# A fused attention and mixture-of-experts kernel: VectorE makes the last block's digits and squares, its rows are loaded in quarters, and the last transposes stand ahead of two down projections

## The reference

```python
y = _moe_mlp(hidden_states, sg_w, su_w, sd_w)
for i in range(E):                                    # E = 16, K = D // 2 = 96
    gate_feature = hidden_states * pe[i] @ gate_w + gate_b
    gate_weight, gate_idx = jax.lax.top_k(gate_feature, K)
    gate_weight = jax.nn.softmax(gate_weight, axis=-1)
    gathered = jnp.take_along_axis(hidden_states, gate_idx, axis=-1)
    y = y + _moe_mlp(gathered * gate_weight, eg_w[i], eu_w[i], ed_w[i])
yn = layernorm(y) * ln_g + ln_b
return jax.nn.silu(yn @ m1_w + m1_b) @ m2_w + m2_b    # added to the residual outside
```

## Time and profile before

| | us |
|---|---|
| median of 3 runs | 2607.87 |
| lowest and highest of them | 2597.53, 2609.46 |
| the profiled execution, its time | 2605.05 |
| the profiled execution, its span | 2603.2 |

### The profile page before, as it was taken

The page is one execution under the profiler, slowest core; times in us unless marked ns, Lnnn a source line. Parts: engine busy times, 40 slices in busy tenths (PEclk is TensorE's granted clock), DMA queues, the critical chain, the costliest instruction groups (busy, mean ns, idle before and its releaser), DMA issues.

```text
span 2603.2 us, 48218 instructions
## 1 busy us (share of the span) xinstructions
PE 2285.7 (88%) x11466; PEld 1244.9 (48%) x11466; DVE 2494.4 (96%) x13314; ACT 1701.2 (65%) x4090; POOL 1791.9 (69%) x2165
## 2 busy tenths in 40 slices
PE   6788989999988889889998889899889988887888
PEld 4555545454444454445544445445445454443445
DVE  5897999999999999999999999999999999999983
ACT  3354676776776667676667767667676666666563
POOL 1245777777786677777767777767768777676683
PEclk8688999988999799999899999998998988989798
DMA  3021222222221222221222122222221222121211
GB/s 107 18 56 27 53 52 61 46 50 55 53 62 44 47 58 46 57 56 44 53 52 61 45 53 50 57 50 56 51 53 49 46 50 61 43 57 46 50 50 26
DMA packets 124767, 133.58 MB, mean 51 GB/s; under 512 B 39923, under 2 KB 112638, under 8 KB 124486
## 3 DMA queue, kind: packets, MB, share of 16 engines
q1 hardware_dynamic: 123174, 128.02, 21.1%
q0 software_dynamic: 880, 1.62, 0.2%
q10 hardware_dynamic: 432, 0.86, 0.1%
HBM read 102.58 MB, written 27.87 MB: 50 GB/s over the span
## 4 chain that ended last, share of the span: by engine, by line
DVE 74%; PE 12%; DMA 4%; POOL 4%; ACT 3%; issue 3%; SPq 0%; DVEq 0%; ACTq 0%; POOLq 0%
DVE idx L647 26%; DVE keys L649 25%; DVE vals L643 22%; PE ps L1281 3%; DMA rows<-digit_d 2%; PE ps L1338 1%; PE ps L1362 1%; DMA digit_d<-dcode 1%; PE ps L1294 1%; PE ps L1245 1%; PE ps L1269 1%; POOL picked L1113 1%; ACT code L834 1%; DVE nmax L593 1%; PE ps L1335 1%
## 5 line engine op out<-in xcount | busy, mean ns | idle before, releaser
L1113 POOL TENSOR_TENSOR picked<-looked_s,code 128x384 f32<-128x384 f32 (+1 forms) x896 | 878.9, 990 | 456.6 <-ACT looked_s L844 455.2
L647 DVE FIND_INDEX8 idx<-vals,keys 128x8 uint16<-128x192 f32 x2712 | 943.2, 349 | 0.0
L844 ACT ACTIVATE looked_s<-ps 128x384 f32<-128x384 f32 (+1 forms) x896 | 440.6, 492 | 653.6 <-PE ps L1281 651.6
L649 DVE MATCH_REPLACE8 keys<-vals,keys 128x192 f32<-128x192 f32 x2486 | 843.4, 339 | 0.0
L643 DVE MAX8 vals<-keys 128x8 f32<-128x192 f32 x2712 | 822.3, 343 | 19.3 <-ACT keys L793 19.3
L1281 PE MATMUL ps<-code,table 128*128 128x384 f32 (+1 forms) x1824 | 839.0, 544 | 0.0
L834 ACT ACTIVATE code<-ps 128x768 f32<-128x768 f32 (+1 forms) x896 | 725.7, 810 | 69.1 <-PE ps L1269 60.4
L1269 PE MATMUL ps<-rows,codew 17*128 17x384 bf16 (+1 forms) x1824 | 320.1, 348 | 189.3 <-ACT code L834 115.0
L1269 PEld LDWEIGHTS ps<-rows,codew 17*128 17x128 bf16 x1824 | 86.9, 92 | 744.8 <-ACT code L834 374.7
L1281 PEld LDWEIGHTS ps<-code,table 128*128 128x128 f32 x1824 | 315.3, 205 | 190.6 <-issue 147.6
L1338 PE MATMUL ps<-xwt,wexp 96*96 96x128 f32 x1792 | 270.8, 299 | 35.9 <-ACT xwt L800 33.6
(11 more groups left out here) (166 smaller groups left out, 2228.3 us busy)
## 6 DMA issues: line engine op xcount, KB each, us to landing
wexp<-in_w_exp SPq DMA_DIRECT2D x58, 576.0 KB, 4.3
wdown<-in_w_down SPq DMA_DIRECT2D x58, 576.0 KB, 4.5
digit_d<-dcode SPq DMA_DIRECT2D x56, 384.0 KB, 2.6
rows<-digit_d SPq DMA_DIRECT2D x224, 96.0 KB
table<-norm_d SPq DMA_DIRECT2D x448, 3.0 KB
patch<-in_patches SPq DMA_DIRECT2D x16, 108.0 KB, 4.7
norm_d<-hs SPq DMA_DIRECT2D x16, 84.8 KB
tok_d<-h SPq DMA_DIRECT2D x16, 84.8 KB
```

The source lines that it names most:

```text
L647: found = nc.vector.max_index(idx[:, par, e, at], vals[:, par, e, at], from_keys[:, e, :])
L649: nc.vector.match_replace(from_keys[:, e, :], vals[:, par, e, at], from_keys[:, e, :], NEG).then_inc(chain, 1)
L844: nc.scalar.activation(looked_s[:, o % 4, 0:w], ps[:, LOOK_B[o % 2], 0:w], ACT.Copy).then_inc(looked_out, 1)
L1113: nc.gpsimd.tensor_tensor(picked[:, o % PICKS, w], looked_s[:, o % 4, w], code[:, o % 4, 1, w], ALU.mult).then_inc(picked_ready, 1)
```

## The change

For the last block only:

- VectorE makes the digits itself in `close_block`: a copy of the low digit to bf16, a subtraction, and one instruction for both squares. ScalarE's two copies and GpSimd's two operations are left out for it.
- ScalarE no longer runs `prepare(LAST)` at octet 8 of block LAST-1. It negates the largest values (`ntop`) at octet `PREPARE_LAST` = 12 behind a wait for `ranked`, and takes the four exponentials in the four steps after that.
- SP loads the rows in 16 DMAs of 24 KB instead of 4 of 96 KB, in the order of the quarters, each quarter with a semaphore of its own, and `make_code` waits for the quarter of its octet.
- PE's `turn_x(LAST)` stands ahead of the two down projections in the code above.

```diff
-PREPARE = 8
+PREPARE, PREPARE_LAST = 8, 12
...
+                    if n < LAST:
...
+                    else:
+                        for x in range(OCT // QUADS):
+                            for a in range(2):
+                                for k in range(2):
+                                    at = code_base(n, a) + PER * k
+                                    sp.dma_start(rows[at:at + PER, x:OCT:QUADS, :],
+                                                 digit_d[n % 2, a, k].rearrange("(o t) c -> t o c", o=OCT)[:, x:OCT:QUADS, :]
+                                                 ).then_inc(rows_last[x], 16)
...
                     nc.vector.tensor_scalar(digits[:, 0:many * TOP], src, LO - 1, None, ALU.bitwise_and).then_inc(ranked, 1)
+                    if n == LAST:
+                        dve.wait_ge(ranked, n + 1)
+                        dve.wait_ge(digits_out, 16 * n)
+                        nc.vector.tensor_scalar(dcode[:, 1, 1, :], digits[:], 1.0, None, ALU.mult).then_inc(parted_last, 1)
+                        dve.wait_ge(parted_last, 1)
+                        nc.vector.tensor_tensor(dcode[:, 0, 1, :], src, dcode[:, 1, 1, :], ALU.subtract).then_inc(parted_last, 1)
+                        dve.wait_ge(parted_last, 2)
+                        nc.vector.tensor_tensor(dcode[:, :, 0, :], dcode[:, :, 1, :], dcode[:, :, 1, :], ALU.mult).then_inc(coded, 1)
...
-                    if o == PREPARE and n < LAST:
+                    if o == PREPARE and n < LAST - 1:
                         prepare(n + 1)
-                    if o > PREPARE and o - PREPARE <= experts_of(n + 1) and n < LAST:
+                    if o > PREPARE and o - PREPARE <= experts_of(n + 1) and n < LAST - 1:
                         exponentials(n + 1, o - PREPARE - 1)
+                    if n == LAST - 1 and o == PREPARE_LAST:
+                        act.wait_ge(ranked, LAST + 1)
+                        nc.scalar.activation(ntop[:, LAST % 2, :], vals[:, LAST % 2, :, 0], ACT.Copy, scale=-1.0).then_inc(negated, 1)
+                    if 0 < step - OCT * (LAST - 1) - PREPARE_LAST <= GRP:
+                        exponentials(LAST, step - OCT * (LAST - 1) - PREPARE_LAST - 1)
...
-                    if o == PREPARE and n < LAST:
+                    if o == PREPARE and n < LAST - 1:
                         square(n + 1)
...
-                    if o == 0:
+                    if n == LAST:
+                        pe.wait_ge(rows_last[octet(o) % QUADS], 64)
+                    elif o == 0:
                         pe.wait_ge(rows_in, 64 * n + 64)
...
                 put(LAST, OCT // QUADS - 1)
+                turn_x(LAST)
                 for step in range(AFTER - DOWN_LAG, AFTER):
                     if step in UNIT_AT:
                         down(*UNIT_AT[step])
-                turn_x(LAST)
```

More of the change, by code:

```diff
@@ L383, in build @@
         plain, ranked, coded, digits_out, rows_in = sem("plain"), sem("ranked"), sem("coded"), sem("digits_out"), sem("rows_in")
-        negated, parted = sem("negated"), sem("parted")
+        negated, parted, parted_last = sem("negated"), sem("parted"), sem("parted_last")
+        rows_last = [sem(f"rows_last_{x}") for x in range(OCT // QUADS)]
         inverted, weights_ready = sem("inverted"), sem("weights_ready")
@@ L494, in slot @@
                         sp.wait_ge(code_done, OCT * n - OCT)
[L495 to L499, removed]
+                    if n < LAST:
+                        for a in range(2):
+                            for k in range(2):
+                                at = code_base(n, a) + PER * k
+                                sp.dma_start(rows[at:at + PER, :, 0:w],
+                                             digit_d[n % 2, a, k].rearrange("(o t) c -> t o c", o=OCT)[:, :, 0:w]).then_inc(rows_in, 16)
+                    else:
+                        for x in range(OCT // QUADS):
+                            for a in range(2):
+                                for k in range(2):
+                                    at = code_base(n, a) + PER * k
+                                    sp.dma_start(rows[at:at + PER, x:OCT:QUADS, :],
+                                                 digit_d[n % 2, a, k].rearrange("(o t) c -> t o c", o=OCT)[:, x:OCT:QUADS, :]
+                                                 ).then_inc(rows_last[x], 16)
                     for i in stored_before(n):
```

## The result

| | median, us | runs | lowest to highest |
|---|---|---|---|
| before | 2607.79 | 20 | 2597.53 to 2615.29 |
| after | 2597.83 | 20 | 2594.59 to 2609.08 |

The ratio is 0.9974, 95% interval 0.9964 to 0.9984: 6.8 us faster (4.2 to 9.4), less than the 0.5% set as the bound of faster, and told from no change only by the number of runs. This ratio is not the quotient of the two medians: they lie 10.0 us apart, which would be 0.9962, outside the interval. So the size of the gain is known only to some 3 us. The profiled execution has a time of 2600.56 us and a span of 2598.7 us.

What follows compares the result with a forecast made beforehand. VectorE's top-k loop was taken to bound the kernel, so only the tail could move: 3.7 us at the last block + 1.3 us behind it = 5.0 us, median 2602.9 us; own range 2600.5 to 2605.5, whole range 2596 to 2608.

Steps and rivals of the forecast that it cites:

- rival A: At the last block: no half-rate stretch, 8.3 us faster, 2599.6; 2597 if clock also holds in last experts; chance 0.25.
- The two paths to the last block: PE's own and the digits' both lead to the last block's first code at 2544.36, 0.9 us apart; the change shortens both.
- the clock: Behind PE's wait for rows at the last block, a half-rate stretch of 6.6 us gives back 2.3 us net.
- PE's own path: Before the last block: without ScalarE's stop at octet 8, PE reaches its code at 2528.18 + 7.10 + 0.81 = 2536.1.
- The digits' path: Digits and squares on VectorE before the last block: 1.7 us undisturbed replaces 3.51 us; coded at 2532.5.
- The hold: GpSimd's work delays VectorE's new operations before the last block, charged once at 0.6 us.
- Quarters: Last block's row loads: PE starts 3.25 us after the first issue, at 2538.4, where whole rows took 7.10 us.
- Rival B: At the last block's first code: quarters come no earlier than whole rows, gain 0.6 us, 2607.3; chance 0.15.
- Start of the last block: PE waits 2.3 us for rows and starts the last block at 2538.4 instead of 2544.36, 6.0 us earlier.
- The moved transposes: After the last block: last expert matmuls start earlier than 2581.32, gain 1.3 us (bounds 0.6 and 1.9).
- Rival C: Before the last block: GpSimd holds all four VectorE operations, rows come 3.2 us late, 2609.8; chance 0.05.

Runs made afterwards that it cites:

- no_turn: The whole change without the moved transposes, against the kernel before: ratio 0.9991 (0.9974 to 1.0007).
- digits_alone: The kernel before with only VectorE's digits and squares and ScalarE's later preparation; rows loaded whole, transposes where they were: ratio 1.0017 (0.9996 to 1.0037).
- after_again: The whole change run once more, unaltered, against the kernel before: ratio 0.9973 (0.9961 to 0.9986).
- filled_tail: The kernel before, order unchanged, with twelve more unused identity transposes between the two last down projections: ratio 0.9987 (0.9977 to 0.9997).
- after_third: The whole change run a third time, unaltered, against the kernel before: ratio 0.9973 (0.9956 to 0.9991).

## Why the prediction came out as it did

The forecast was 5.0 us faster, the measured 6.8 by the ratio (4.2 to 9.4). The median, 2597.83, lies below the forecast's own range of 2600.5 to 2605.5, between rival A's two figures (2599.6, and 2597 with the clock up in the last experts), and inside the whole range of 2596 to 2608, which took in A's lower end. The two paths to the last block and the ways to shorten them were as told; the clock was rival A's in two of three executions. Term by term:

- *PE's own path* (7.10 + 0.81 us from octet 10's look): exact, 2535.72 to 2543.6, and 7.10 us from look to look in the two other executions of the change too. What was off is where PE stands against the digits: its look for octet 10 started 1.8 us ahead of the digits in the execution that I read, and 0.7 us behind, 1.3 ahead and 0.8 ahead in those of the change.
- *The digits' path*: 1.7 us undisturbed was near the 1.6 us with GpSimd paused. The hold, one of 0.6 us in the sum, was 0.9 to 2.2 us over the three executions of the change (store issued at 2.48, 2.78, 3.71 us instead of 1.56), 2.5 us with `no_turn`, which has the same digits, and 4.0 us with `digits_alone`. Mechanism right, size too small; the early store that this part promised, 1.2 us, came out as 0.1 to 1.3, and as 0.3 us late in `no_turn`.
- *Quarters*: 3.25 us from first issue to PE; 2.78, 2.77, 2.75 measured. The half-size row was a fair guide. Rival B is refuted: four transfers of 24 KB let PE start 4.3 us sooner than four of 96 KB. The rule of the Trainium skill (DMA: Bandwidth & Descriptors, Bandwidth) on transfers under 64 KB speaks of efficiency; here latency of the first part was wanted, and 16 loads together were issued in 5.44 us behind work of PE that hid them.
- *Start of the last block*: 6.0 us earlier forecast; 5.3, 6.2 and 6.6 measured.
- *The clock*: this step failed in two executions of three. I gave 2.3 us back for a half-rate stretch behind a wait for rows of 2.3 us. The waits were 0.56, 1.54 and 0.72 us, since PE arrived later against the digits than in the execution I had read; behind the 1.54 us the clock fell and the last block took 34.5 us, 2.1 more than before, near my 2.3; behind the other two it stayed up and the block took 32.3 us. Rival A described these, and its 8.3 us lie inside the interval, but its 1.0 us from the full clock did not come: 32.3 us is 0.1 less than the 32.4 of before. In the forecast half of a half-rate stretch was its price, since PE seemed to bound the block; at full clock PE is busy 31.0 of 33.4 us, and the 6.8 us of half rate in `after_again` (2 x 3 x (0.35 + 0.50 + 0.29), from the three rows shown for it) cost 2.2, not some 3.4 us. Behind all waits for rows of 3.8 us and more (five executions) the clock fell and the block took 34.5 to 36.4 us.
- *The moved transposes*: 1.3 us forecast, 4.2 us measured (22.0 to 22.3 us from the scaling to the end in seven executions, against 26.4 to 26.7 in five of the six without; the sixth, 23.2, kept its clock and shows the 1 us of waiting alone). The 1.3 us of waiting were right (3.25 against 4.54 us); the other 2.9 us are the last experts at full clock, which the sum left out without a reason and only rival A had, as some 2.5 us. `filled_tail` says that it is the idling and not the order, with one profile and an interval that ends at 0.9997.
- *Rival C*: the hold exists, its largest of 3.3 us on one instruction exceeds the 2.46 us that I took from a row, but only one or two of the four instructions were held in an execution, and together it never reached the 7.3 us that would have turned the sign.

Without the 2.3 us that it took off for the clock, and with the 2.9 us that it left out, the forecast would have been 10.2 us; the three tails of the change (63.6, 65.0 and 62.5 us) are 9.6, 8.3 and 10.8 us shorter than the 73.3 us of the execution that I read. That 5.0 us lies inside the measured interval is in part luck, since the tails say about twice as much. What stays open is how large the gain is: the ratios say 7 us in all three groups, the medians 10.0, 6.4 and 7.6, the tails 8 to 13. The rest of an execution varies by more than that difference, the half-rate stretches come and go, and two or three profiles of each kernel can't say whether the tails of all of them are so far apart. Nor was `digits_alone` repeated, whose 3.53 us hold may be an unlucky one.

## What to carry to other kernels

When two paths of nearly equal length end at one instruction, see which one holds in several executions before paying for either: the digits' part with the free run of ScalarE gained nothing alone (1.0017), and even with the rows in quarters its own gain is not shown (0.9973 against 0.9983). Split a load whose first part is wanted first, even into transfers of 24 KB, if the rest is hidden behind work. And look for what is idle in front of the last dense stretch of matmuls: a wait of 1.7 us there mostly cost another 2.9 us in clock, and moving ready work ahead of it gave back that and 1.3 us of waiting.

## What the hardware did that I had not expected

- GpSimd held VectorE's digit operations, of one input and of two, for as long as it ran without a gap: a 0.26 us copy took 3.53 us, a 0.36 us subtraction 1.20 us beside a pick that began 0.01 us earlier. The timelines of `after_third`:

```profile
2533.01 1.20 DVE L640 TENSOR_TENSOR dcode<-idx,dcode 128x384 bf16<-128x384 uint16 x1
2534.24 0.56 DVE L642 TENSOR_TENSOR dcode<-dcode 128x768 bf16<-128x768 bf16 x1
```
```profile
2533.00 1.00 POOL L1136 TENSOR_TENSOR picked<-looked_s,code 128x384 f32<-128x384 f32 x1 [0.44 <-ACT looked_s L862]
2534.45 0.94 POOL L1066 TENSOR_TENSOR prod_s<-gu_s 96x256 f32<-96x256 f32 x1 [0.46 <-ACT gu_s L909]
```

  So the two-input form, which no row before showed, is hit too, as the Trainium skill (GPSIMD Engine Reference, Specifications) has it. The square started in GpSimd's gap and went through in 0.56 us, and GpSimd's product beside it took 0.94 instead of 0.72 us: in both pairs the one that started second took longer.
- A quarter of the rows, 96 KB in four DMAs, let PE start 2.75 to 2.78 us after the first issue, where half the bytes took 4.55 and all took 7.1.
- PE's clock fell behind 1.72 us of idling and a few light microseconds, in five of six executions, and stayed up where 1.21 us of idling stood in its place (seven of seven).
